# Transformer layer with expert-choice feed-forwards on one core: attention results turned on VectorE, a planned order for TensorE, and reordered early rows and last block of the feed-forward

## The reference, cut to what matters

```python
def ffn(h):                       # h = layernorm(x): [2, 2048, 256]
    scores = softmax(h @ gate_w.T).transpose(0, 2, 1)      # 16 experts
    topk_w, topk_idx = top_k(scores, 256)                  # per batch and expert
    g, u = x_tok @ Wg, x_tok @ Wu                          # x_tok: the 256 chosen tokens
    out = scatter_add((gelu(g) * u @ Wd) * topk_w)
    return out + gelu(h @ Ws_g) * (h @ Ws_u) @ Ws_d        # shared expert, all tokens
def attn(h):                      # 16 heads of 16 features, rotary positions, causal
    p = softmax(mask(q @ k.T / 4))
    return (p @ v) @ Wo.T + bo
x = x + 0.5 * ffn(layernorm(x)); x = x + attn(layernorm(x)); x = x + 0.5 * ffn(layernorm(x))
```

## Time and profile before

| | |
|---|---|
| median of 3 runs | 1736.07 us |
| profiled execution | 1735.24 us |
| its span, first to last instruction | 1733.5 us |
| TensorE busy (share) | 1557.6 us (90%) |
| ScalarE busy | 1021.4 us (59%) |
| VectorE busy | 864.1 us (50%) |
| GpSimd busy | 566.1 us (33%) |
| mean granted TensorE clock | 0.961 |

### The profile page before, as it was taken

The page is one execution under the profiler, slowest core; times in us unless marked ns, Lnnn a source line. Parts: engine busy times, 40 slices in busy tenths (PEclk is TensorE's granted clock), DMA queues, the critical chain, the costliest instruction groups (busy, mean ns, idle before and its releaser), DMA issues. The chain is left out here.

```text
span 1733.5 us, 26994 instructions
## 1 busy us (share of the span) xinstructions
PE 1557.6 (90%) x10135; PEld 1087.0 (63%) x10137; DVE 864.1 (50%) x1854; ACT 1021.4 (59%) x1423; POOL 566.1 (33%) x480
## 2 busy tenths in 40 slices
PE   4899899999975858999999999998489989999996
PEld 3788788888864633333333333343378878989885
DVE  5787557676735740112221121322578756666673
ACT  6322344454515747999999999997642234454541
POOL 2000056666545871111121011110200015665644
PEclk9999999999997977999999999999699999999999
DMA  8131056666634797224225056000812115666753
GB/s 284 28 104 49 25 158 152 156 152 153 131 37 167 214 249 144 46 30 75 35 41 75 17 97 136 1 13 25 287 35 98 49 32 155 160 148 151 155 126 37
DMA packets 120755, 183.31 MB, mean 106 GB/s; under 512 B 19440, under 2 KB 83056, under 8 KB 117360
## 3 DMA queue, kind: packets, MB, share of 16 engines
q1 hardware_dynamic: 91440, 130.17, 29.4%
q0 software_dynamic: 29184, 51.40, 14.2%
HBM read 125.95 MB, written 55.57 MB: 105 GB/s over the span
## 5 line engine op out<-in xcount | busy, mean ns | idle before, releaser
L1708 ACT ACTIVATE 8046_pr<-8046_pS 128x1024 f32<-128x1024 f32 x448 | 423.8, 1072 | 36.2 <-PE 8046_pS L1620 35.8
L1650 PE MATMUL 8046_pO<-8046_pr,6228_vres 128*32 128x512 f32 x1792 | 240.2, 608 | 7.1 <-DVE 8046_oT L1731 6.0
L1620 PE MATMUL 8046_pS<-sq_rows,sk_rows 50*128 50x512 f32 x896 | 190.7, 474 | 23.5 <-DMA sq_rows<-shift 20.6
L1620 PEld LDWEIGHTS 8046_pS<-sq_rows,sk_rows 50*128 50x128 f32 x896 | 77.5, 186 | 206.8 <-ACT 8046_pr L1708 136.8
L168 PE MATMUL 88_pGU<-columns_XT,weights_wts 128*128 128x512 f32 x384 | 152.7, 398 | 2.5 <-DVE 88_hf L826 1.3
L168 PE MATMUL 15040_pGU<-columns_XT,weights_wts 128*128 128x512 f32 x384 | 152.5, 397 | 2.5 <-DVE 15040_hf L826 1.3
L1722 POOL TENSOR_SCALAR_AFFINE_SELECT 8046_pr<-8046_pr 128x512 f32<-128x512 f32 x32 | 20.3, 635 | 397.8 <-ACT 8046_pr L1708 397.8
L169 PE MATMUL 88_pGU<-columns_XT,weights_wts 128*128 128x512 f32 x384 | 150.1, 391 | 0.0
L169 PE MATMUL 15040_pGU<-columns_XT,weights_wts 128*128 128x512 f32 x384 | 150.1, 391 | 0.0
L170 PE MATMUL 88_pGU<-columns_XT,weights_wts 128*128 128x512 f32 x384 | 150.0, 391 | 0.0
L170 PE MATMUL 15040_pGU<-columns_XT,weights_wts 128*128 128x512 f32 x384 | 150.0, 391 | 0.0
(11 more groups left out here) (310 smaller groups left out, 3430.3 us busy)
## 6 DMA issues: line engine op xcount, KB each, us to landing
token_table<-weights_xn POOLq DMA_DIRECT2D x16, 512.0 KB, 6.3
88_raw_g<-WgT SPq DMA_DIRECT2D x16, 512.0 KB
88_raw_u<-WuT SPq DMA_DIRECT2D x16, 512.0 KB, 3.7
88_raw_d<-WdT SPq DMA_DIRECT2D x16, 512.0 KB, 4.2
q_rows<-rows_half SPq DMA_DIRECT2D x32, 256.0 KB, 3.4
k_rows<-rows_half SPq DMA_DIRECT2D x32, 256.0 KB, 3.6
sq_rows<-q_rows SPq DMA_DIRECT2D x32, 256.0 KB
sk_rows<-k_rows SPq DMA_DIRECT2D x32, 256.0 KB
```

What stands on the lines that cost most here:

```text
L1620: m = t_.matmul(to[:, e, :], key, query, start=True, stop=True)
L1650: m = t_.matmul(pO[e * 32:(e + 1) * 32, off:off + wd], vres[:, (g // GB) * TPB + kt, at:at + 32], from_(e), start=n == first[j], stop=n == ...
L1708: s_exp.done(a.activation(to, pS[:, u % RING, :, :], ACT.Exp, scale=HD ** -0.5))
```

## The change

Feed-forward: the loads of quads 0 and 1 of the first feed-forward are issued in the constants' block, quad 0 ahead of the constants, into SBUF at a fixed place (`first_x`); the shared weights are loaded between quads 1 to 3 and split in steps 3 to 5; VectorE's low columns lag three steps, not two; the first expert's weights are loaded after the softmax; `spread_rows` moves from hook "d" to hook "c" of `down(J, 0)`, the list of rows ahead of `low(J, 3)` on VectorE; `down(J+1, 1)` goes ahead of the turns; in the last `down` six of its sixteen products go ahead of the wait for the last quarter of the hidden values.

Attention: VectorE transposes pO in 32x32 blocks from PSUM to SBUF, divides into `yb`, whose layout is now that of blocks, and transposes again in 32x32 blocks when the half is complete; Wo's rows and V's bias are put in that order by the host, V's bias is added for each partition in the split. TensorE's turns and "A" are gone. TensorE's table is made by a budget, in units of 10 ns, for each exponential. The last block is turned, divided and split in halves; the last pieces go into the score buffers. SP's loads and stores keep their order. `start` is gone: with this table the first split of the second batch, (4, 0), comes in step 347 and its first piece in step 350, and four pieces are left for the end: (6, 1) and (7, 1).

```diff
@@ load_constants, on SP
+                load_x(0)
                 sp.dma_start(self.ident[:, :], self.ins["c_ident"]).then_inc(s_id, 16)
...
+                for q in range(1, EARLY):
+                    load_x(q)
@@ ffn, on SP
-                load_x(0)
-                load_x(1)
-                for w in range(3):
-                    s_raw[w].done(sp.dma_start(raw[w][:, :, :], shared_src[w]))
-                for q in range(2, J):
-                    load_x(q)
+                for q in range(J):
+                    if q >= first:
+                        load_x(q)
+                    if 1 <= q <= 3:
+                        s_raw[q - 1].done(sp.dma_start(raw[q - 1][:, :, :], shared_src[q - 1]))
                 load_residual(0)
                 load_residual(1)
+                sp.wait_ge(*s_soft.at(B))
                 for w in range(3):
-                    sp.wait_ge(*s_wls.at(w + 1))
+                    s_wls.wait(sp, w + 1)
...
@@ down, on TensorE
+                    early = [(q, c) for q in (0, 2) for c in range(FC - 1)] if last else []
...
+                    s_ev.wait(t_, 2 * (d - 1) + (2 if last else h + 1))
+                    order = [(q, c) for q in (2 * h, 2 * h + 1) for c in range(FC) if (q, c) not in early]
+                    if h == 0:
+                        order = early + order
@@
                 down(J + 1, 0)
+                down(J + 1, 1)
                 turn(J, 0)
                 turn(J, 1)
-                down(J + 1, 1)
@@ VectorE, early rows
-                    if q >= 2:
-                        low_columns(q - 2)
+                    if q >= 3:
+                        low_columns(q - 3)
@@ attention, TensorE's table
+            EXP, PAIR, VALUE, PIECE = 90, 34, 25, 90
+            while len(slot) < len(items):
+                spent = max(spent, EXP * (w - 1)) + (PAIR if w + RING < NU else 0)
+                more = True
+                while more and len(slot) < len(items):
...
+                    until = unit_of[2 * (s + NR)] - 2 if what == "whole" and s + NR < len(whole) else NU
+                    more = known[n] <= w and (spent + wide * VALUE // 2 <= EXP * (w + 1) or w >= until)
+                    if n == first[j] and j:
+                        more = more and w >= slot[-1] + 2
...
+                if len(piece_at) < len(pieces) and not waits and spent + PIECE // 2 <= EXP * (w + 1):
+                    m, c, r = pieces[len(piece_at)]
+                    j = last_of(m, c)
+                    if len(slot) > final[j]:
+                        if r == 0:
+                            begin = max(free + 1, slot[final[j]] + 1)
+                            if w >= begin + 3:
+                                split_at[begin] = (m, c)
+                                piece_at[w] = (m, c, r)
...
@@ attention, VectorE
+                def turn(j, part=slice(0, 512)):
+                    v.wait_ge(*s_O.at(final[j] + 1))
+                    s_y.wait(v, j)
+                    s_copy.done(v.transpose(tO[:, part], pO[:, part]))
...
+                    s_yq.done(v.transpose(yq[:, part], flat(yb[:, c, m % QB, :, :])[:, part]))
+                    v.wait_ge(*s_yq.at(k + 1 + again))
+                    s_yT.done(v.tensor_scalar(yT[0][:, part], yq[:, part], bias_v[:, c:c + 1], None, ALU.add))
...
+                    if n in split_at:
+                        m, c = split_at[n]
+                        if c == 0:
+                            with_bias(m)
+                        split(m, c)
```

More of the change, by code:

```diff
@@ L221, in _, with ffn @@
                 dve.wait_ge(s_cast, 3)
-    def ffn(self, x, out):
+    def ffn(self, x, out, first=0):
         nc, ALU, ACT, AX, bass = self.nc, self.ALU, self.ACT, self.AX, self.bass
@@ L1517, in attention @@
-            quads = [(m, 0) for m in range(4)] + [(m, 1) for m in range(4)] + [(m, 0) for m in range(4, 8)] + [(m, 1) for m in range(4, 7)]
-            U8 = NU // NG
-            for n, (m, c) in enumerate(quads):
-                bb, qb = m // QB, m % QB
-                ready = max(at_turn[(bb * GB + 2 * c + k) * QB + qb] for k in range(2)) + 2
-                start = {0: 2, 4: 4, 8: 6}.get(n)
-                if start:
-                    at = max(at, start * U8 + 6)
-                at = max(at, ready)
-                pace = 10 if n < 8 else 6
-                for r, piece in enumerate((("A", 0), ("B", 0), ("B", 1))):
-                    side[at] = (m, c, *piece)
-                    at += pace
@@ L1530, in attention @@
-            assert len(side) == 45
-            order = []
-            for n in range(NW):
-                if n in side:
-                    order.append(side[n])
-                for j in turn_at.get(n, ()):
-                    order.append(("T", j))
-            late = [(m, c, *piece) for m, c in ((7, 1),) for piece in (("A", 0), ("B", 0), ("B", 1))]
-            assert max(side) < NW
-            order += late
-            place = {what: n for n, what in enumerate(order)}
-            assert len(place) == len(blocks) + 48
@@ L1542, in attention @@
-            splits = [w_ for w_ in order if len(w_) == 4 and w_[2] == "A"]
-            split_no = {w_[:2]: n for n, w_ in enumerate(splits)}
+            quads = ([(m, c) for c in range(DC) for m in range(QB)] + [(m, c) for c in range(DC) for m in range(QB, 2 * QB)])
+            last_of = lambda m, c: ((m // QB) * GB + 2 * c + 1) * QB + m % QB
+            pieces = [(*mc, r) for mc in quads for r in range(2)]
+            place = {what: n for n, what in enumerate(pieces)}
+            EXP, PAIR, VALUE, PIECE = 90, 34, 25, 90
@@ L1545, in attention @@
+            NW = w
+            late = pieces[len(piece_at):]
+            ends_at = {slot[final[j]]: j for j in range(len(blocks))}
             s_w, s_b = sig("attn_w", 16), sig("attn_bias", 16)
+            at_end = lambda m, c, r: pS[:, late.index((m, c, r)) % RING, late.index((m, c, r)) // RING, :]
             s_xin = [sig(f"attn_x{k}", 16) for k in range(4)]
             s_out = [sig(f"attn_out{k}", 16) for k in range(4)]
-            s_S, s_O, s_side = (sig("attn_pe_" + n_) for n_ in ("S", "O", "side"))
+            s_S, s_O, s_piece = (sig("attn_pe_" + n_) for n_ in ("S", "O", "piece"))
@@ L1685, in _ @@
                         n += 1
-                    if w in side:
-                        project(*side[w])
-                    for j in turn_at.get(w, ()):
-                        turn(j)
+                    if w in piece_at:
+                        project(*piece_at[w])
                 assert n == len(items)
@@ L1789, in _ @@
                         s_wh.done(v.tensor_tensor(wo[1][:, :, :], raw[:, :, :], wo[0][:, :, :].bitcast(f32), ALU.subtract))
-                    for j in copy_at.get(n, ()):
-                        copy(j)
-                    if n in side:
-                        project(*side[n])
-                    for j in turn_at.get(n, ()):
-                        heads_of(j)
+                    if n in ends_at and ends_at[n] < len(blocks) - 1:
+                        turn(ends_at[n])
+                        heads_of(ends_at[n])
+                    if n in piece_at:
+                        add(*piece_at[n])
+                    if n in split_at:
[3 more added lines that the diff above has]
+                        split(m, c)
+                for m, c in quads:
+                    if (m, c, 0) in late and (m, c) != quads[-1]:
+                        split(m, c)
+                j = len(blocks) - 1
+                for again in range(2):
+                    turn(j, slice(256 * again, 256 * again + 256))
+                for again in range(2):
+                    heads_of(j, slice(8 * again, 8 * again + 8), again)
+                    split(*quads[-1], slice(256 * again, 256 * again + 256), again)
                 for piece in late:
-                    project(*piece)
+                    add(*piece)
     def attn(self, x, out):
```

217 lines of the change are left out of this document (107 added, 110 removed).

## The result

The changed kernel takes 1709.25 us, the median of 4 runs (1705.94 to 1715.88), against 1735.03 before (4 runs, 1733.30 to 1738.00): ratio 0.9855, 95% interval 0.9839 to 0.9872. Forecast was 1695, range 1664 to 1712. It is faster, by 25.8 us where 40.5 were forecast. Run again beside other runs of before (1735.44), the same kernel gave 1701.85 (1696.74 to 1704.83), ratio 0.9802, interval 0.9769 to 0.9835: its own times spread over 19 us, more than those of before (11), and the slowest run of the second set (1704.83) is faster than the fastest of the first (1705.94).

The account below looks back on a forecast made before the run. In attention TensorE and ScalarE were both near the bound; without turns, ScalarE would set the pace. Attention's 14.7 us (24 lost in a stall) and the feed-forwards' 25.8 gave 40.5 off 1735.2: 1695, own range 1684 to 1708, wide 1664 to 1712.

Parts of the forecast that it names:

- rival B: Steady attention: TensorE stays the bound, half the gaps outlive the turns; gain 15 us, not 32, so 1712; chance 14%.
- the stall: Second batch's start: TensorE waits at step 350 for residual(4), queued behind a late store; 24 us lost.
- Attention, steady: Attention from 691 us on: without turns ScalarE sets the pace, 473 us plus 8 left over; 32 us gained, less 1.
- The transposes: VectorE's transpose of pO in the copy's place: 0.7 us each, covered at block ends, so no cost.
- Piece 78: Attention, first split of a pair with the residual's bias: about 1 us late for this piece, 1 us lost.
- Start of attention: First block: no more wait for the broadcast bias, now needed only at step 75; 5.7 us gained.
- rival A: Second batch's start: residual(4) isn't late, so the 24 us aren't lost; 1671 us; chance 20%.
- End of attention: Last exponential to the next block: turn, division and split in halves take 7.7 us against 10.1; 2 us gained.
- Early rows: Both feed-forwards' first rows: lag of three ends VectorE's wait, 6.0 and 5.6 us; earlier start in the first, 2.8 more.
- Where the experts begin: Change from shared to routed: earlier list and eight products ahead of the turn, so TensorE doesn't stand; 4.6 us each.
- Last down: End of each feed-forward: six early products fill a 2.23 us wait, scatters start 1.1 us earlier; 1.1 us each.
- Rival C: Attention's block ends: VectorE's transpose out of PSUM is slow, TensorE waits; 2.8 us each eats all 40; chance 3%.

Follow-up runs that it names:

- e1: The changed kernel with store(0..3) and residual(4..7) behind the heads of g = 5 on SyncE, not g = 6, one wake earlier: 1681.96 us, ratio 0.9708.
- e5: The changed kernel with VectorE's transpose of pO done twice, the second waiting for the first: 1719.61 us, ratio 0.9901.
- e6: The changed kernel with four more 128x256 products on TensorE at each block's start, overwritten by the true ones: 1713.23 us, ratio 0.9869.
- e2: The changed kernel with stores and residuals ahead of the heads of g = 6 at the same wake, not behind them: 1685.93 us, ratio 0.9713.
- e10: The changed kernel with batch two's first split no earlier than step 380 in TensorE's table, SyncE's list unchanged: 1682.02 us, ratio 0.9704.
- e7: The changed kernel with four, not six, early products in the last down, then a wait for the third quarter: 1701.0 us, ratio 0.9813.

## Why the prediction was right or wrong

The direction was right and the first time lies inside the range of 1664 to 1712, but the number alone would have misled: 1709.25 is nearer to rival B's 1712 than to my 1695, and just outside my own 1684 to 1708; 1701.85 of the second set is inside. What upholds the forecast is the mechanism, term by term. Some luck is in the total too: the stall cost 3 us less than I gave it, which hides most of the 4 us that the steady part lacked.

- **Attention, steady: 31 forecast, 26.7 measured** (e1, exponentials 29 to 544: 488.1 us against 514.8). The mechanism was right: no turns, and block ends that wait 0.2 us each. The mis-sized term is the allowance for what is left, 8 us over 473; it measured 15. About 2 of them are a miscount of mine: the two windows of the earlier trace rows add up to 516 exponentials, but two of them lie across the border at 1000 and are counted twice, so 514 share the time: one costs 0.920 and not 0.916, and 516 cost 475. Of the rest e1 has 9.6 us of waits in 21 gaps, each with the 0.11 of the prediction beside its length, 2.3; about 1 is left over. TensorE's "slack of 19" isn't a reserve that a wait can draw on (e5, e6).
- **The transposes: 0 forecast, little measured**; 0.70 us forecast, 0.716 measured; TensorE waited 3.6 us for them in all (1.9 for the copies before, from 688 us on). The estimate of 1.24 us by the Trainium skill ("VectorE: DVE Perf Modes", The three transpose paths; its 311 ns is for a 128x128 bf16) is not borne out for this fp32 tile: 0.716 decides.
- **Piece 78: 1 forecast, 1.86 measured.** The same wait stood at step 350 once the stall was gone; the two are 3.7 of e1's 9.6 us.
- **Start of attention: 5.7 forecast, 7.8 measured.** No wait for the bias is left.
- **The stall: 24 forecast, 21 measured**, its place, its chain and its landing within 1.4 us (e1, e2, e10). Without it (e1) the time is 1682; rival A had 1671, since it carried my other terms' errors.
- **End of attention: 2 forecast, -0.3 and 0.1 measured.** The chain from the last exponential's end to the last addition's end was to be 2.4 us shorter and became 1.6 (11.2 to 9.5); the last store cost the 0.4 forecast. But the next block's first load took 5.2 us and not 3.8 till its statistics. My sum had nothing for it. The stores had landed by then, so it isn't they; the cause is open.
- **Early rows: 6.0 and 8.4 forecast, 6.5 and 7.4 measured** (second and first feed-forward). Another 1.4 us came in the first feed-forward between the early rows and the rank product, for which the sum had no term.
- **Where the experts begin: 4.6 each forecast; -0.2 and -0.7 in the first profile, 4.7 and 3.9 in the second.** The step was right where the turn came on time: TensorE doesn't stand ahead of it, and the columns' bare way measured 1.64 us (1.7 forecast). What the sum had at nothing is a late hand-over: with the columns' way bare, the turn's 2.1 us and what followed it made TensorE's stand 2.9 us longer, and the half clock behind that cost 2.0 us more. In both feed-forwards that is 9.4 us, more than the whole difference between the two profiled executions (1706.9 and 1699.2).
- **Last down: 1.1 each forecast, -0.3 measured** (second feed-forward). "Six products fill the 2.23" was wrong: they need the third quarter, which VectorE makes 0.8 us ahead of the fourth, and three of them delay the first half, whose end starts the scatters (e7).

Rival B (the steady part still TensorE's, 1712) was refuted by the gaps, 21 of them with 8 us, where it wanted over 15, though e6 shows that its price was half right. Rival C needed 2.8 us a transpose by my sum; by e5's 0.60 us lost for each 0.75 it would eat the changed kernel's 26 us at about 0.72 + 26 / (31 x 0.8) = 1.8 us (an estimate), so it was nearer than I thought.

## What to carry to other kernels

A table that moves work earlier must be read against every queue that feeds it: a guard such as `start` may be the only sign that a transfer lands late, and moving the transfer to an earlier wake brings the same as the guard. Slack summed over a stage pays for little at one step (here 0.15 to 0.2 us of 0.75). Products moved away from a hand-over over two engines leave it bare: what the new order wins in most executions (1.8 us each here) it loses in one where the hand-over is late, so judge it over several.

## What the runs showed of the hardware that was not expected

The semaphore of a TensorE group came later than its recorded (modelled) end: 2.1 us at one place, in both feed-forwards of one execution and in none of ten others with the same code there. A transpose of 128x512 fp32 in 32x32 blocks on VectorE took 716 ns out of PSUM and 704 ns out of SBUF; a copy of the same size out of PSUM had 692. A store of 512 KB landed within 3.4 us with nothing ahead of it, and in 16.6 us behind the heads' transfers, with the DMA engines busy all the time. TensorE's granted clock fell to 0.50 in a stand of 4.54 us and stayed at 1.00 through one of 1.64.
